# The second feed-forward's hidden chunks in pairs, with four GELU buffers and a newly planned order of the whole program

## What is computed

```python
h = x @ down_w + down_b                       # 256 -> 128
gate = softmax(top two of softmax(x @ router_w + ...))
out = 0
for k in range(2):                            # the two chosen experts of each row
    for e, (w1, b1, w2, b2) in enumerate(experts):   # hidden sizes 128,256,384,512,128,256,384,512
        hm = h * mask[k, e]
        acc += gelu(gelu(hm) @ w1 + b1) @ w2 + b2
    out += acc * gate[k]
out += 0.1 * (gelu(gelu(h) @ shared_w1 + shared_b1) @ shared_w2 + shared_b2)
x = x + out @ up_w + up_b + gelu(x) @ core_w + core_b
```

## Time and profile before

| | |
|---|---|
| median of 3 runs | 417.0 us (416.74, 417.00, 418.52) |
| the profiled execution | 420.97 us, span 419.2 us |
| TensorE busy | 373.0 us (89%), 3768 instructions |
| VectorE busy | 235.2 us (56%) |
| ScalarE busy | 221.3 us (53%) |
| GpSimd busy | 93.3 us (22%) |
| mean granted clock of TensorE | 0.935 |

### The profile page before, as it was taken

The page is one execution under the profiler, slowest core; times in us unless marked ns, Lnnn a source line. Parts: engine busy times, 40 slices in busy tenths (PEclk is TensorE's granted clock), DMA queues, the critical chain, the costliest instruction groups (busy, mean ns, idle before and its releaser), DMA issues.

```text
span 419.2 us, 9361 instructions
## 1 busy us (share of the span) xinstructions
PE 373.0 (89%) x3768; PEld 302.9 (72%) x3768; DVE 235.2 (56%) x611; ACT 221.3 (53%) x419; POOL 93.3 (22%) x173
## 2 busy tenths in 40 slices
PE   3355939999999999997999999899998999996896
PEld 1343838888888877987778888588876888775574
DVE  4798494869587447788344212855348036436242
ACT  2344832654654555595684312667644236775662
POOL 7872112322123032310001334000053120002000
PEclk9975776999999999997999999699999999999699
DMA  9990000000000000000000000000000000000000
GB/s 190 410 396 11 2 0 2 2 2 2 2 2 0 3 2 2 2 2 0 2 3 27 2 0 1 2 1 2 14 16 1 2 0 2 3 2 25 0 2 26
DMA packets 8218, 12.16 MB, mean 29 GB/s; under 512 B 4464, under 2 KB 6768, under 8 KB 7408
## 3 DMA queue, kind: packets, MB, share of 16 engines
q1 hardware_dynamic: 8176, 11.57, 8.3%
HBM read 10.52 MB, written 1.05 MB: 28 GB/s over the span
## 4 chain that ended last, share of the span: by engine, by line
PE 73%; DVE 16%; ACT 5%; issue 3%; POOL 2%; POOLq 0%; DVEq 0%; ACTq 0%
PE Y L1226 23%; PE H L1226 22%; PE S L1226 15%; PE S L1267 4%; PE S L1327 3%; PE S L1291 1%; PE S L1234 1%; DVE PT L990 1%; DVE MN L989 1%; ACT A L778 1%; PE S L1243 1%; PE S L1392 1%; ACT L778 1%; DVE K L976 1%; DVE KT L1057 1%
## 5 line engine op out<-in xcount | busy, mean ns | idle before, releaser
L1226 PE MATMUL H<-XT,WF 128*128 128x256 f32 x256 | 62.5, 395 | 0.0
L869 POOL TENSOR_TENSOR A<-R 128x512 f32<-128x512 f32 x32 | 33.3, 1039 | 125.8 <-PE Y L1226 74.9
L1226 PE MATMUL Y<-WP,A 128*128 128x256 f32 x256 | 59.5, 382 | 0.0
L1226 PE MATMUL H<-GH,W 128*128 128x256 f32 x168 | 50.6, 407 | 7.1 <-ACT GH L769 4.2
L778 ACT ACTIVATE A<-H,B 128x256 f32<-128x256 f32 x84 | 38.9, 475 | 32.1 <-PE Y L1226 22.7
L1226 PEld LDWEIGHTS H<-XT,WF 128*128 128x128 f32 x256 | 49.0, 198 | 8.4 <-ACT R L752 0.8
L1226 PEld LDWEIGHTS Y<-WP,A 128*128 128x128 f32 x256 | 47.3, 190 | 6.1
L1226 PE MATMUL Y<-A,W 128*128 128x256 f32 x168 | 50.5, 397 | 0.2 <-ACT A L778 0.2
L752 ACT ACTIVATE R<-H 128x512 f32<-128x512 f32 x32 | 19.1, 597 | 46.2 <-PE H L1226 46.1
L1226 PEld LDWEIGHTS H<-GH,W 128*128 128x128 f32 x168 | 30.7, 199 | 14.4 <-ACT A L778 5.9
L1180 DVE TENSOR_TENSOR YG<-YS,Y 128x256 f32<-128x256 f32 x32 | 13.4, 420 | 39.1 <-ACT YS L795 39.0
(11 more groups left out here) (183 smaller groups left out, 647.1 us busy)
## 6 DMA issues: line engine op xcount, KB each, us to landing
W<-in_w SPq DMA_DIRECT2D x2, 1344.0 KB, 11.0
WF<-in_wf SPq DMA_DIRECT2D x2, 1024.0 KB, 7.8
WP<-in_wp SPq DMA_DIRECT2D x2, 1024.0 KB, 9.8
X<-in_x SPq DMA_DIRECT2D x8, 128.0 KB, 8.4
out_dram<-X SPq DMA_DIRECT2D x8, 128.0 KB, 1.7
CD<-in_ctx_in SPq DMA_DIRECT2D x2, 256.0 KB, 5.4
C<-in_ctx_in SPq DMA_DIRECT2D x1, 256.0 KB, 2.9
CT<-in_ctxT SPq DMA_DIRECT2D x1, 256.0 KB, 3.9
```

The costliest lines, as they stand in the source:

```text
L869: nc.gpsimd.tensor_tensor(flat(A0[:, n % 2, :, :]), R0[:, n % 2, :], R0[:, n % 2, :], ALU.mult).then_inc(a0_ready, 1)
L1226: return nc.tensor.matmul(o, a, b, start=start, stop=stop, skip_group_check=shared)
```

## The change

- The chunks of step c go in pairs (11 steps in place of 21): `up1` writes two chunks into the two halves of one H bank, `hidden` runs two GELUs and signals once, after the second.
- `A1` has four buffers in place of two: a GELU waits for the down product four chunks back, not two.
- The product with `selG` that spreads an expert's gates stands behind its last chunk.
- The experts go by size: the shared one, then those of 4, 4, 3, 3, 2, 2, 1 and 1 chunks; before, by number (1, 2, 3, 4, 1, 2, 3, 4).
- The planner has new numbers: the costs of c, `SWITCH` 5.3 to 4.2, `CHANGE` 8.0 to 1.8, all `SLACK` and all `URGENCY`.

```diff
-EXPERTS = [E1] + list(range(E1))
+EXPERTS = [E1] + sorted(range(E1), key=lambda e: -CH1[e])
...
-SWITCH = 5.3
-CHANGE = 8.0
-SLACK = {"pe": 0.039, "act": 0.052, "dve": 0.154, "pool": 0.024}
+SWITCH = 4.2
+CHANGE = 1.8
+SLACK = {"pe": 0.18, "act": 0.0, "dve": 0.14, "pool": 0.1}
...
-           "zero": (-347.7, 19.6), "constg": (-587.6, 61.3), "constm": (64.6, -29.8), "consti": (-58.3, 210.5)}
+           "constm": (-52.9, 20.4), "consti": (-248.5, 148.8)}
...
-        A1, YS, YG = A0[:, :, 0, :], sb("YS", [P, 2, GT], fp32), sb("YG", [P, 2, GT], fp32)
+        A1, YS, YG = A0[:, :, :, :].rearrange("p a b s -> p (a b) s"), sb("YS", [P, 2, GT], fp32), sb("YG", [P, 2, GT], fp32)
...
             def hidden(g, i):
-                e, c = WORK[i]
-                n = g * NCH1 + i
                 b, done = filled(act, "ffn1", g, "c", i)
-                if n >= 2:
-                    chunk_used(act, n - 2)
-                ch = FIRST1[e] + c
-                nc.scalar.activation(A1[:, n % 2, :], b[:, 0:GT], ACT.Gelu, bias=B1[:, ch:ch + 1]).then_inc(done, 1)
+                pair_ = range(2 * i, min(2 * i + 2, NCH1))
+                for k, w in enumerate(pair_):
+                    e, c = WORK[w]
+                    n = g * NCH1 + w
+                    if n >= 4:
+                        chunk_used(act, n - 4)
+                    ch = FIRST1[e] + c
+                    ins = nc.scalar.activation(A1[:, n % 4, :], b[:, k * GT:(k + 1) * GT], ACT.Gelu, bias=B1[:, ch:ch + 1])
+                ins.then_inc(done, 1)
...
-                mm(b[:, 0:GT], W1[:, FIRST1[e] + c, :], GH[:, :]).then_inc(done, 1)
+                for k, (e, c) in enumerate(WORK[2 * i:2 * i + 2]):
+                    ins = mm(b[:, k * GT:(k + 1) * GT], W1[:, FIRST1[e] + c, :], GH[:, :])
+                ins.then_inc(done, 1)
...
-                    if e < E1:
-
-                        mm(b[:, GT:2 * GT], selG[:, e, :], GTT[:, :])
-                last_c = c == CH1[e] - 1
-                ins = mm(at(*y)[:, 0:GT], W2[:, FIRST1[e] + c, :], A1[:, (g * NCH1 + i) % 2, :], start=(c == 0), stop=last_c)
-                ins.then_inc(full["Y"] if last_c else a1_used, 1)
+                    ins = mm(at(*y)[:, GT:2 * GT], selG[:, e, :], GTT[:, :])
+                ins.then_inc(full["Y"], 1)
```

More of the change, by code:

```diff
@@ L36 @@
 BLOCKS0 = E0 * K0 // 2
-EXPERTS = [E1] + list(range(E1))
+EXPERTS = [E1] + sorted(range(E1), key=lambda e: -CH1[e])
 WORK = [(e, c) for e in EXPERTS for c in range(CH1[e])]
+PAIRS1 = (NCH1 + 1) // 2
 def stages(part, n, *names):
@@ L73 @@
     "ffn1": dict(v="dve 1.53 pool .7", ln="dve .77", x="pe .45 act .59", i="pool 1.43", r="pe .9 dve .59",
-                 e="act .2 dve 1.5", t="act .2 dve 2.0", d="pe .87 act 1.13", g="pe .13 act .36", c="pe .43 act .47",
+                 e="act .2 dve 1.5", t="act .2 dve 2.0", d="pe .87 act 1.13", g="pe .13 act .36", c="pe .86 act .94",
                  w="pe .43", y="act .47 dve .88", o="pe 1.3 dve .42", b="act .22", z="pe 1.12 dve .16")}
@@ L91 @@
 BODY = {("ffn0", "u"), ("ffn0", "d"), ("ffn0", "y"), ("ffn1", "c"), ("ffn1", "w"), ("ffn1", "y"), ("ffn1", "o")}
-URGENCY = {"attn0": (38.7, 20.0), "attn1": (-9.9, 32.6), "attn1_keys": (-23.0, -18.9),
-           "ffn0": (-33.7, 4.9), "ffn0_body": (-114.2, -4.5), "ffn1": (669.6, -114.4), "ffn1_body": (-36.9, 30.7),
-           "zero": (-347.7, 19.6), "constg": (-587.6, 61.3), "constm": (64.6, -29.8), "consti": (-58.3, 210.5)}
+URGENCY = {"attn0": (42.5, 11.6), "attn1": (41.4, 49.2), "attn1_keys": (44.2, -21.8),
+           "ffn0": (76.2, -151.4), "ffn0_body": (-227.1, 108.7), "ffn1": (365.5, -236.3),
+           "ffn1_body": (23.3, 64.3), "zero": (-286.1, 25.8), "constg": (-883.6, 145.5),
+           "constm": (-52.9, 20.4), "consti": (-248.5, 148.8)}
 BODIES = [("ffn0", 0)] + [x for g in range(GROUPS - 1) for x in (("ffn0", g + 1), ("ffn1", g))] + [("ffn1", GROUPS - 1)]
@@ L102, in work_of @@
         e, c = WORK[s[3]]
-        if c == 0 and e < E1:
+        if c == CH1[e] - 1 and e < E1:
             parts = [("pe", parts[0][1] + GATE)]
+    if s[0] == "ffn1" and s[2] == "c" and 2 * s[3] + 1 == NCH1:
+        parts = [(e, d / 2) for e, d in parts]
     if s[0] == "ffn1" and s[2] == "y" and s[3] == 0:
@@ L223, in ffn1 @@
         for i, (e, c) in enumerate(WORK):
-            add(f("c", i), f("d"))
-            add(f("w", i), f("c", i))
-            if c == 0 and e == EXPERTS[1]:
+            if i % 2 == 0:
+                add(f("c", i // 2), f("d"))
+                if i >= 4:
+                    need(f("c", i // 2), f("w", min(i + 1, NCH1 - 1) - 4), part=1)
+            add(f("w", i), f("c", i // 2))
+            if c == CH1[e] - 1 and e == EXPERTS[1]:
                 need(f("w", i), f("g"))
@@ L232, in ffn1 @@
                     need(f("y", j), f("z", E1 // 2 - 1))
-            if i >= 2:
-                need(f("c", i), f("w", i - 2), part=1)
         for k in range(2):
@@ L1473, in down1 @@
                 y = ("ffn1", g, "y", EXPERTS.index(e))
-                read_out(pe, "ffn1", g, "c", i)
+                read_out(pe, "ffn1", g, "c", i // 2)
                 if c == 0:
-                    b, _ = claim(pe, *y)
+                    claim(pe, *y)
+                last_c = c == CH1[e] - 1
+                ins = mm(at(*y)[:, 0:GT], W2[:, FIRST1[e] + c, :], A1[:, (g * NCH1 + i) % 4, :], start=(c == 0), stop=last_c)
+                if not last_c:
+                    ins.then_inc(a1_used, 1)
+                    return
+                if e < E1:
                     if e == EXPERTS[1]:
```

## The result

The changed kernel takes 411.94 us (median of 4 runs, 410.17 to 412.72), the kernel before 417.11 us in the same comparison (4 runs, 416.74 to 418.52): ratio 0.9864, 95% interval 0.9825 to 0.9903. In a second comparison it was 412.98 against 417.05, ratio 0.9885 (0.9822 to 0.9949). It is faster by 1.4% (5.2 us; by the ratio of the second comparison 1.2%), where 2.2% (9 us) were forecast; 411.9 lies inside the range of 401 to 416.

The account below looks back on a forecast made before the run. TensorE bounds the kernel, busy 373 of 419.2 us, plus its idle time and low clock. Terms -3.4 -3.1 -3 -3 +2.1 +0 +1.4 = -9.0 took the profiled 420.97 to 412, carried to the median 417.0: 408; range 401 to 416.

Parts of the forecast that it names:

- the lead is carried: Whole kernel: TensorE starts its dense part 6 to 7 us ahead and nothing gives it back; 400 to 411 us, chance 0.55.
- 340 to 385: Stretch at 340 to 385 us: wait for `ACC` gets cover, last row transposes get a wait; 0, bounds -1.5 and +1.5.
- Row transposes earlier: Opening: the first feed-forward's row transposes start near 57 us instead of 60.4; -3.4 us, bounds -5 and -1.
- Work already done: Opening: three of four zero rows move into TensorE's waiting time, with other work shifted; -3.1 us, bounds -2 and -3.6.
- Clock in the opening: Ahead of the row transposes: the hole shrinks to some 2 us, so less low clock follows; -3 us, range -1.9 to -5.3.
- 180 to 201: Stretch at 180 to 201 us: zero-row bank wait goes, TensorE work covers VectorE's query splitting; -3 us, bounds -5.8 and +2.
- rival 2: Lead half eaten: TensorE waits for VectorE and ScalarE, the hole at 180 to 201 stays; 411 to 415 us, chance 0.25.
- Borders and new waits: Behind the opening: 21 new array-mode borders at 0.1 us cost +2.1; disorder from 71.5 to 180 us costs +1.4.
- Last body: Last body: waits per four chunks and single-chunk experts offset gains at the head and hand-overs; 0, bounds -2 and +2.5.
- Rival 3: Fours of the bodies: pairs make TensorE wait for ScalarE, +18 us there, about 424 us in all; chance 0.09.

## Why the prediction was right or wrong

The direction was right; the size was 4 us too large. Of the likeliest rival (the lead is carried) half is right: no engine that feeds TensorE ate the lead (only 340 to 385 gave 1.4 us back), but the lead was not 6 to 7 us. The first hidden pair starts at 178.26 for 180.41, 2.15 us earlier, where some 7 were named as a sign. Most of the gain came behind that point. Step by step:

**The sum against the profile.** -9.0 was forecast against the profiled 420.97, giving 412; the profiled execution after took 412.72. **The step that failed is carrying this difference to the median.** I subtracted it from 417.0 as though the median run of before lost as much to the clock as the profiled one. It lies 4.0 under that one, and the runs above show that one and the same list differs by 2.8 us with the clock's pattern in the opening and by 1.7 at 317. In the runs beside the experiments, those of the kernel before with the profiled one's mean clock of 0.935 took 420.8 to 420.9 us, nearly all others 415.5 to 419. So part of what I took away, the median run no longer had. Which pattern it had, no profile shows; this last point is inferred. That the sum of the terms came within 0.8 us of the profiles' difference is in part luck, since terms missed in both directions. (The losses that it starts from are seven places, not the six it says; the sum doesn't use the count.)

**Row transposes earlier, -3.4.** Measured -2.54; in the two profiles of the same list with the other clock pattern `XN` stands at 56.84 and 56.90, which is the forecast. The steps were only in part as worked. The first root came at 8.04 as said, and the moved root alone gives 1.2. But VectorE's last score piece ended at 42.22 and not at 39.4, and the key copy at 44.73 and not at 42.2: VectorE wasn't 4 us ahead. TensorE was through by 52.5 (52 forecast) because the clock, in the profiled run, was full there, where 3.3 us were reckoned for a low one. Two misses cancelled. And 1.6 of the 2.54 are the queries' wait that no longer stands in front of `XN`.

**Work already done, -3.1.** The zero rows do stand in the opening, but not free: putting them back made `XN` 1.8 to 2.8 us earlier. Their worth lies in the next term.

**Clock in the opening, -3.** Measured: nothing. I had written that the bank's wait may bring the clock down; it did, and the clock was low from 54 to 68 us, 14 us as before. Neither a moved read nor added products brought a gain that a median shows.

**180 to 201, -3.** With the zero rows that left, this was the largest item: -5.7 together, and the stage from `DW` 0 to `DW` 1 got 4.73 us shorter. The wait for the splitting of the queries, which rival 2 feared, did not come. My bound of 5.8 counted the same time twice: a clock of 0.84 costs only while TensorE is busy. And the price of the zero rows in that place, 9.3 us when they are put back, was beyond both of my bounds.

**Borders and new waits, +2.1 and +1.4.** From `XN` to `DW` 0 the two kernels take the same, 115.87 and 115.69 us, though the changed one has about 2.3 us less attention work in it, an estimate from the two lists (some is done ahead of `XN`, some comes behind `DW`). Between 68 and 178 us there is no idle time (109.91 of 110.0 busy). The 0.60 us idle between 57.9 and 68 and, at 0.1 us each, 13 further borders would make 1.9 of it; this is argued, since no run changed the borders alone.

**340 to 385, 0.** The stage from `DW` 2 to `DW` 3 got 1.44 us longer, at the end of my bound: TensorE waits 1.00 us for `XN` and 0.77 for `XT`, where before it waited 1.20 for `ACC`.

**Last body, 0.** Measured -2.06, at my lower bound. A round of four chunks lost 0.27 and 0.16 us in the two that were read and not 0.35, the last `UW` waits 0.25 instead of 0.69, and the wait of 2.00 us in the head is gone. The sign named for this stretch was 21.4 us from the first product behind the first GELUs to the last down product; it was 18.7 (385.24 to 403.96), since two more chunks were up by then (0.9 us) and, by my estimate for the rest, because the clock was low up to 395 us before and up to 386 now. Rival 3 did not come: there is no wait over 0.5 us for a GELU in the first three bodies. Its price was also added up too low: 15 waits of 1.35 us are 20.3, not 18.

## What to carry over

A filler step's place decides, not its length: three zero rows in front of a closed bank cost 9 us, and 2 to 3 in an opening that waits anyway. Before a saving is counted, ask whether the matrix engine bounds the stretch behind: a hole or a low clock costs only there, and the cheapest find was a wait with ready work right behind it in the list, which two moved steps took away. When a forecast is made from one profiled execution, carry its difference to the median only for terms that don't hang on the clock.

## What the runs showed of the hardware

- A wait of 2.20 us at the same place, in nearly the same list, was followed by a low clock in four profiles and not in six; and one opening list ran with the clock low from 54 to 68 us (four profiles) or from 17 to 41, 55 to 58 and 62 to 65 (two). The spread of this kernel's times (0.6% either way) is of the size of these two. With the hole at 317 gone, the six runs of each kernel lie within 0.35 and 0.46%.
- VectorE's 128x2 and 128x16 instructions at 313.78 and 315.48 took 0.97 and 1.01 us, others of that size 0.17. GpSimd worked at those very times:

```profile
313.69 1.04 POOL L877 TENSOR_TENSOR A<-R 128x512 f32<-128x512 f32 x1 [5.21 <-PE Y L1234]
315.42 1.04 POOL L877 TENSOR_TENSOR A<-R 128x512 f32<-128x512 f32 x1 [0.69 <-PE Y L1234]
```

Both VectorE instructions end within 0.04 us of the GpSimd one. In these two places the gates' chain takes 1.6 us longer, in front of a 2.20 us wait of TensorE. The Trainium skill ("SBUF — State Buffer", section SBUF: two separate sides) says that VectorE and GpSimd share one pair of ports under an exclusive lock: whichever starts first has it for the whole instruction and the other is fully blocked, if the VectorE instruction runs in a 2-port mode or has two inputs in SBUF. The times agree with such a block; that the first of the two instructions meets the condition, the trace doesn't show. No run moved the GpSimd work to test it.
